# Row-tiled attention scores issued one batch pair ahead, with the odd units' softmax split over ScalarE and GpSimd

## The reference, cut to what matters

```python
x -> x + tanh(g_xattn[l]) * attention_l(layernorm(x), ctx)
x -> x + tanh(g_ffn[l])   * ffn_l(layernorm(x))          # layer 0: shared + top-1 of 8 experts; layer 1: two LoRA experts

scores = einsum('bhqd,bhkd->bhqk', Q, K) / sqrt(8)       # layer 1 adds a 64x64 bias and a key mask
attn = softmax(scores, -1)
out = einsum('bhqk,bhkd->bhqd', attn, V) @ Wo.T
```

## Time and profile before

| | us |
|---|---|
| median of 3 runs (lowest, highest) | 190.31 (189.04, 190.61) |
| the profiled execution, its own time | 189.79 |
| its span, first to last instruction | 188.0 |
| attention of layer 0 on DVE, unit 0 to the last norm before the tail | 13.58 to 55.5 |
| expert stage and what lies around it | 55.5 to 121.95 |
| attention of layer 1 on DVE, the same | 121.95 to 158.0 |
| rest of layer 1 (up- and down-projection, output) | 158.0 to 188.0 |

### The profile page before, as it was taken

The page is one execution under the profiler, slowest core; times in us unless marked ns, Lnnn a source line. Parts: engine busy times, 40 slices in busy tenths (PEclk is TensorE's granted clock), DMA queues, the critical chain, the costliest instruction groups (busy, mean ns, idle before and its releaser), DMA issues.

```text
span 188.0 us, 4325 instructions
## 1 busy us (share of the span) xinstructions
PE 171.0 (91%) x1606; PEld 94.8 (50%) x1606; DVE 145.8 (78%) x364; ACT 79.9 (43%) x178; POOL 78.4 (42%) x88
## 2 busy tenths in 40 slices
PE   8768599999998979899998969989999998998994
PEld 2234236555576446366665923333555555643593
DVE  0599997889989799385666496799989996869942
ACT  3253284664473342255554002245544556255300
POOL 8729991004043864005666603255674454110000
PEclk9999969999999999999999997999999999999999
DMA  6999999940002010444421030000000000000012
GB/s 158 321 420 362 257 239 247 207 137 2 3 0 24 29 58 31 89 105 91 78 51 31 6 111 4 0 2 2 3 0 3 0 3 0 3 0 0 3 40 71
DMA packets 19558, 15.01 MB, mean 80 GB/s; under 512 B 3493, under 2 KB 18087, under 8 KB 19282
## 3 DMA queue, kind: packets, MB, share of 16 engines
q1 hardware_dynamic: 18370, 13.17, 27.9%
q0 software_dynamic: 736, 1.07, 1.8%
q10 hardware_dynamic: 432, 0.50, 1.1%
HBM read 7.82 MB, written 6.85 MB: 78 GB/s over the span
## 4 chain that ended last, share of the span: by engine, by line
PE 53%; DVE 26%; issue 7%; DMA 5%; POOL 5%; ACT 2%; SPq 0%; DVEq 0%; POOLq 0%
PE bank L877 44%; PE bank L954 6%; DMA xr<-x_in 3%; POOL rstd L311 3%; DVE oT L640 2%; DVE Sa L633 2%; DVE xn L585 2%; POOL Sx L384 2%; DVE st L566 2%; PE bank L1193 2%; DVE Vx L606 2%; DVE mx L635 2%; DMA sorted_rows<-Pe,slot 1%; DVE QT L614 1%; DMA big<-sorted_rows 1%
## 5 line engine op out<-in xcount | busy, mean ns | idle before, releaser
L877 PE MATMUL bank<-Kx,QT 128*64 128x512 f32 x128 | 34.9, 629 | 2.6 <-DVE Sx L626 2.0
L311 POOL TENSOR_TENSOR rstd<-ve,nhalf 128x2 f32<-128x2 f32 x16 | 11.7, 728 | 54.1 <-DVE ve L572 54.0
L461 ACT ACTIVATE Pe<-Sx 128x512 f32<-128x512 f32 x32 | 20.2, 630 | 27.3 <-POOL Sx L384 15.1
L954 PEld LDWEIGHTS bank<-cst,Pe 128*128 128x128 f32 x128 | 13.8, 143 | 25.1 <-issue 14.6
L372 POOL DMA_INDIRECT routed_rows<-big x15 | 14.8, 984 | 19.3 <-DVE big L842 12.2
L465 ACT ACTIVATE big<-bank 128x512 f32<-128x512 f32 x32 | 18.8, 587 | 8.5 <-PE bank L954 8.2
L954 PE MATMUL bank<-cst,Pe 128*128 128x128 f32 x128 | 21.4, 291 | 0.7 <-ACT Pe L461 0.6
L384 POOL TENSOR_TENSOR Sx<-Sa,mx 128x512 f32<-128x512 f32 x16 | 16.8, 1049 | 11.3 <-DVE mx L635 11.3
L640 DVE RECIPROCAL oT<-bank 128x128 f32<-128x128 f32 x16 | 15.3, 953 | 3.7 <-PE bank L877 3.6
L877 PE MATMUL bank<-zb 128*32 128x512 bf16 x47 | 15.5, 473 | 2.5 <-DVE bo L597 1.4
L414 ACT ACTIVATE xn<-xr,nmr,rstd 128x128 f32<-128x128 f32 x20 | 9.1, 486 | 16.0 <-DVE nmr L578 16.0
(11 more groups left out here) (110 smaller groups left out, 302.9 us busy)
## 6 DMA issues: line engine op xcount, KB each, us to landing
sorted_rows<-empty SPq DMA_DIRECT2D x1, 4686.0 KB, 29.0
wgu<-rgu SPq DMA_DIRECT2D x1, 2048.0 KB, 10.6
wdn<-rdn SPq DMA_DIRECT2D x1, 1024.0 KB, 12.6
big<-sorted_rows SPq DMA_DIRECT2D x15, 66.0 KB, 1.9
ctxT<-ctx_in SPq DMA_DIRECT2D x2, 256.0 KB, 4.7
xr<-x_in SPq DMA_DIRECT2D x2, 256.0 KB, 5.3
wf<-ffn SPq DMA_DIRECT2D x1, 512.0 KB, 4.4
Kx<-KT SPq DMA_DIRECT2D x16, 32.0 KB
```

The costliest lines, as they stand in the source:

```text
L311: pool.tensor_tensor(rstd[:, w], ve[:, w], nhalf[:, w], ALU.pow).then_inc(s_pow, 1)
L461: act.activation(Pe[:, u % 3, :], Sx[:, u % 2, :], ACT.Exp).then_inc(s_exp, 1)
L877: return pe.matmul(o, l, r, start=first, stop=last, **k)
L954: ins = pe.transpose(bank[2 + u % 2][:, m * P:(m + 1) * P], Pe[:, u % 3, m * P:(m + 1) * P], ident)
```

## The change

**Scores.** K is now kept in four copies (`Kx` [P, 4, T]) and Q in one (`QT` [P, T]). The 16 heads are four groups of 32 features; a matmul contracts only one group's 32 rows with 256 streamed columns (4 heads). A unit is four such matmuls (two groups by two batches), which lie in different rows and columns of the array. The banks 0 to 3 become two double banks `pair0` and `pair1`; a unit's two groups end in two neighbouring banks, and `heads[i]` is the middle 512 columns.

**Order.** PE issues both units of pair n+1 ahead of the transposes of unit (n-1, odd) and (n, even), then the values of pair n-1 and out_proj of n-2. There is one bank for values, one for out_proj and one for each parity of transposes.

**Even units** are treated as before. **Odd units**: ACT copies the scores to `Sa` (`score_evac`); in layer 1 POOL adds bias and mask in place (`add_bias`); DVE takes the maximum in SBUF (`max_o`); POOL subtracts (`subtract`) in both layers. In layer 1 POOL subtracts for the even units too, as before.

**Other moves.** Both `v_proj` of layer 0 and `out_bias` stand ahead of the first scores. The transposes of xn pieces 2 and 3 and one `q_proj` of 512 columns for both come in iteration 2. The routed rows `xs` have a tile of their own. The last odd unit's transposes come behind `xn_transpose(q, 0)`. One `keep_warm` of two matmuls at the start of attention of layer 1 is gone.

```diff
@@ tensor
+            def scores(layer, n, hh):
+                if n >= 1:
+                    if hh == 1:
+                        pe.wait_ge(s_ev, PAIRS * layer + n)
+                    elif layer == 0:
+                        pe.wait_ge(s_sube, n)
+                    else:
+                        pe.wait_ge(s_adde, n)
+                for g in range(2):
+                    w = slice(32 * (2 * hh + g), 32 * (2 * hh + g + 1))
+                    for r in range(2):
+                        b = 2 * n + r
+                        o = pair[hh][S * r:S * r + S, 256 * (g + 1):256 * (g + 2)]
+                        ins = mm(o.rearrange("p (h k) -> p h k", h=HG), QT[w, b * S:(b + 1) * S],
+                                 Kx[w, :, b * S:(b + 1) * S])
+                ins.then_inc((s_Se, s_So)[hh], 1)
...
             def attention(layer, step):
+                for n in range(-1, PAIRS):
+                    if n < PAIRS - 1:
...
+                        scores(layer, n + 1, 0)
...
+                        scores(layer, n + 1, 1)
+                    if n == 2:
+                        xn_transpose(2 * layer, 2)
+                        xn_transpose(2 * layer, 3)
+                    if n >= 1:
+                        transposes(layer, n - 1, 1)
+                    if n >= 0:
+                        transposes(layer, n, 0)
+                    if n == 2:
+                        q_proj(layer, 2, 2)
+                    if n >= 1:
+                        values(layer, n - 1)
+                    if n == 3:
+                        out_proj(layer, 0)
+                    if n >= 3:
+                        out_proj(layer, n - 2)
+                xn_transpose(q, 0)
...
+                    pe.wait_ge(s_xnT, PIECES * q + 1)
+                    keep_warm(XT_BANK[q][0], 3)
+                    transposes(1, 7, 1)
+                    out_proj(1, 6)
+                    values(1, 7)
+                    xn_transpose(q, 1)
@@ vector
+                for n in range(PAIRS):
+                    unit_e(layer, n)
+                    if n in (4, 6):
+                        add_out(layer, n // 2 - 2)
...
+                    if n >= 2:
+                        norm(layer, n - 2)
+                    max_o(layer, n)
+                    if n == 0:
+                        q_evac(layer, 1)
+                        normalise(2 * layer, 2 + layer)
...
+                    if n == 2:
+                        q_evac(layer, 2, 2)
+                    if n in (4, 6):
+                        out_stats(layer, n // 2 - 2)
@@ gpsimd, layer 1
+            add_bias(0)
+            for n in range(PAIRS):
+                if n >= 1:
+                    subtract(1, n - 1, 1)
+                if n in (2, 3):
+                    residual_base(1, n - 2)
+                if n in (5, 7):
+                    rstd_of(3, (n - 5) // 2)
+                subtract(1, n, 0)
+                if n < PAIRS - 1:
+                    add_bias(n + 1)
+            subtract(1, PAIRS - 1, 1)
@@ scalar
+                for n in range(PAIRS):
+                    if n >= 1:
+                        exp(layer, n - 1, 1)
+                    if layer == 0:
+                        exp(0, n, 0)
+                    if n < PAIRS - 1:
+                        score_evac(layer, n + 1)
+                    if layer == 1:
+                        exp(1, n, 0)
...
+                    if n >= 1:
+                        pt_evac(layer, n - 1, 1)
...
+                    pt_evac(layer, n, 0)
...
+                    if n == 7:
+                        xnT_evac(q, 0)
...
+                            normalise(q, 1)
+                exp(layer, PAIRS - 1, 1)
+                pt_evac(layer, PAIRS - 1, 1)
```

More of the change, by code:

```diff
@@ L763, in attention @@
                 else:
-                    norm(1, 6)
-                    residual(1, 2)
                     norm(1, 7)
@@ L1078, in _ @@
             pe.wait_ge(d_cst, 32)
-            for a in (0, 1):
-                xn_transpose(0, a)
-                q_proj(0, a)
+            xn_transpose(0, 0)
+            q_proj(0, 0)
+            xn_transpose(0, 1)
+            v_proj(0, 0)
+            q_proj(0, 1)
+            v_proj(0, 1)
             def shared_up(n, halves=(0, 1)):
```

438 lines of the change are left out of this document (212 added, 226 removed).

## The result

| | median, us | lowest to highest | executions |
|---|---|---|---|
| before | 190.09 | 188.90 to 191.31 | 20 |
| changed | 191.80 | 190.41 to 193.94 | 20 |

The changed kernel takes 1.0077 times as long as before, 95% interval 1.0046 to 1.0108. Forecast were 186.3 us and a range of 182.0 to 191.3. The sign was wrong, and the time lies outside the range: it is 5.5 us above the forecast. The profiled execution took 192.07, with a span (first to last instruction) of 190.3 us.

What follows compares the result with a forecast made beforehand. PE (91% busy) bounded the kernel, DVE the first pairs of each layer. Span 188.0 - 5.6 + 0.1 + 0.4 + 1.0 = 183.9, plus 1.8 outside and 0.5 for the median: 186.2, said 186.3; range 182.0 to 191.3.

Steps and rivals of the forecast that it cites:

- The scores: PE in attention: a pair's scores take 0.75 us instead of 2.02, with bounds of 0.65 and 2.02.
- Rival B: Row groups do not run side by side, a pair's scores keep 2.02 us; 190.3 to 191.5 us; chance 0.13.
- DVE, ACT and POOL: Work per pair: DVE 3.15 us instead of 3.9, ACT about 2.6, POOL 3.3 in layer 1 with additions at 1.28.
- Rival D: PE remains the bound and the whole saving of 20 us arrives, 170 us; chance 0.02.
- Layer 0: Attention of layer 0: last maximum ends at 48.8 us, last residual at 56.5 instead of 62.1, a gain of 5.6.
- the walk: Step-by-step reckoning of both layers' attention, with pairs at 3.2 us in layer 0 and 3.4 in layer 1.
- the clock term: First pairs of both layers: light PE work brings 1.2 GHz; 1.0 us taken, +2.0 if counted in both layers.
- rival C: Clock stays low as PE waits for POOL or DVE; 3.4 us more per pair, two give 193.1; chance 0.12.
- Layer 1: Attention of layer 1: slow first three pairs, last norm at 154.8 instead of 158.0, tail gives it back; +0.1, addition +0.4.
- list of signs: What the profile after should show, among it layer 1's up-projections about 41 us behind its first unit.
- The Q copy and the tail: DVE gap of about 2 us ahead of the 512-column Q copy; last odd exponential on ACT behind xn's copy and layer norm.

Runs made afterwards that it cites:

- e11: e8 with every score matmul issued three times into the same place; 201.92 us, 1.0656 of the kernel before.
- e13: Changed kernel with idle matmuls on zeros in PE's waits of layer 0 alone (start and tail); 189.77 us, 1.0019 of the kernel before.
- e5: Changed kernel with idle matmuls on zeros in every place where PE waits, those of e1 and later pairs; 187.69 us, 0.9858 of before.
- e8: e7 with one layer norm tile in layer 1's first iteration moved from DVE to ACT; 184.41 us, 0.9692 of the kernel before.
- e1: Changed kernel with idle matmuls on zeros in the starts of both layers and the tail of layer 0; 190.31 us, 0.9977 of before.
- e2: Changed kernel with idle matmuls on zeros in layer 1's start only; 192.03 us, 1.0050 of the kernel before.
- e6: e5 with layer 1's last odd unit let ahead on ACT and PE, as in e4; 186.16 us, 0.9795 of the kernel before.
- e7: e6 with DVE's copy of 512 Q columns moved behind the even unit of pair 3; 184.99 us, 0.9722 of the kernel before.
- e4: Changed kernel with layer 1's last odd exponential and transposes let ahead, no idle matmuls added; 191.10 us, 1.0019 of the kernel before.
- e9: Changed kernel with only the later copy of 512 Q columns on DVE, no idle matmuls added; 190.61 us, 0.9982 of the kernel before.

## Why the prediction was wrong, point by point

**The scores, right.** 0.75 us per pair was taken; 0.61 at full clock. Rival B, no effect of the row tiling, is out by the timeline and by e11.

**DVE, ACT and POOL, right in their sizes.** The addition on POOL takes 1.27, taken at 1.28. In a pair without a residual, DVE's even unit comes 3.11 us after the one before (29.85 to 32.96), forecast 3.2 to 3.5. With a residual it is 5.3 to 6.0 (42.06 to 47.34 and 32.96 to 38.95), where 3.2 + 1.45 and small waits were counted. Rival D, PE stays the bound, is out: PE is busy 81% of the span.

**Layer 0, right except for the clock.** With the clock held the last residual starts at 56.49 (e13), 56.33 (e5) and 55.87 (e8); the walk said 56.5. In the changed kernel it starts at 60.68. Timeline of DVE in the changed kernel:

```profile
49.85 0.68 DVE L714 TENSOR_REDUCE mx<-Sa 128x8 f32<-128x512 f32 x1
...
60.68 0.48 DVE L728 SCALAR_TENSOR_TENSOR xr<-bank,tg,xb 128x256 f32<-128x256 f32 x1 [0.91 <-PE bank L956]
```

The last maximum ends at 50.53, 1.7 after the 48.8 of the walk; from there to the residual it takes 10.2 instead of 7.7. So 1.7 us were lost in the pairs and 2.5 in the tail, where the clock term had nothing. With the clock held both terms of the walk come out: in e5 the last maximum ends at 48.01 + 0.68 = 48.69, and the residual follows 7.6 us later.

**The clock, the step that failed.** It was put at +1.0, at most +2.0, for pair 0 of each layer, because PE's light work was looked for only where the walk showed long waits. Fillers bring back 4.1 us (e5): the term is that size. Three things were missed. The low clock also follows the tail of layer 0, where PE works in small pieces. It lasts longer than one stretch: against rival C stood that PE would be busy nearly all the time at half clock and so get the full clock back, but from 121.8 on in layer 1 PE was busy only 1.12 and 2.47 of 3.40 us at 1.2 GHz, waiting for DVE and POOL, and the low clock went on to 132.1. (the earlier trace rows do not show the clock behind their busy stretch either; the page's row of forty slices does.) And it isn't fixed in place: with PE idle 19% of the span, the low clock appears here or there (e1, e2, e13). Rival C named the right mechanism and gave it 0.12, with a price of 3.4 us for 6.8 us at 1.2 GHz, that is 0.5 us for each. In the later pairs the runs come near that: the 3.4 us stretch of e1 at 145.80 makes the step from unit_e(6) to unit_e(7) 152.82 - 145.44 = 7.4 us instead of 150.46 - 144.59 = 5.9 in e5, 0.4 us for each. In layer 1's start ten us at 1.2 GHz cost only 0.8, because others set the pace there. Over the whole kernel, 24 us cost about 4.1, a third of C's price.

**Layer 1, the second miss.** (unit_e(n) is the even unit of pair n on DVE.) The walk had unit_e(1), unit_e(2) and unit_e(3) 3.6, 6.2 and 13.5 us after the first unit. They came after 5.3, 7.9 and 16.3 (starts at 119.80, 125.06, 127.68, 136.07). From unit_e(3) to the up-projections, 28.3 + 0.4 = 28.7 was forecast, and it took 28.8. So the 2.8 us lie in the first three pairs, and 1.7 of them ahead of unit_e(1). There the clock has no part: in e6, at full clock, unit_e(1) also comes 121.48 - 116.21 = 5.3 us after the first unit. What was in no step of the walk is that POOL holds up two small DVE instructions, 1.05 and 0.80 us over their free durations. Taking one away brings unit_e(1) 1.06 us forward, of which 0.6 to 0.7 reach the end (e8); the other was not taken away in any run. The clock has 16.3 - 15.4 = 0.8: in e6 unit_e(3) comes at 131.64 - 116.21 = 15.4. The remaining 0.3 has no run of its own. The prediction's list of signs had about 41 us for this stage, its own walk 42.2; 45.03 was measured.

**The Q copy and the tail, right, and avoidable.** A gap of about 2 us ahead of the Q copy was forecast; 2.15 and 1.60 were seen, and the exponential behind the copy of xn's transposes too. Both were taken as given by the change. They are an order of instructions, and moving them gives 1.2 and 1.5 us with the clock held (e7, e6).

**The sum.** Of the 5.5 us between 186.3 and 191.8, the clock has about 3.1 (4.1 less the 1.0 that was counted), and the held DVE instructions up to 1.7. The rest, 0.7 or more, no run accounts for: of the one instruction that was moved only 0.6 of 1.06 us reached the time. The range failed for the same reason. Its upper end came from rival B, which does nothing to the clock, and C, which does, was left outside.

| version | us | ratio to before | last residual, layer 0 | first unit to up-projection, layer 1 |
|---|---|---|---|---|
| before | 190.09 | 1 | 62.12 | 40.71 |
| changed | 191.80 | 1.0077 | 60.68 | 45.03 |
| e5, clock held | 187.69 | 0.9858 | 56.33 | 44.83 |
| e6, and tail order | 186.16 | 0.9795 | 56.17 | 42.72 |
| e7, and later Q copy | 184.99 | 0.9722 | 55.96 | 41.93 |
| e8, and a norm tile on ACT | 184.41 | 0.9692 | 55.87 | 41.20 |

**What stays open.** The change as it was made loses 0.8%; with the clock held it gains 1.4%, and with three small moves more 3.1%. No run here tells why the stretch from 53.5 to 56.9, with PE busy in many small matmuls (2.49 of 3.40 us), was followed by 1.2 GHz, since the fillers of layer 0 were only tried together. Nor is it known which fillers of e5 are needed; those of one layer alone (e2, e13) and those of the starts and the tail (e1) bring back 2.0 us at most.

## What to carry to other kernels

When a change takes work from a PE that was nearly always busy (91% here), price the clock as its own term over the whole kernel, and not only at the longest wait: here light work in the two attention stages cost 4.1 us, more than the 2.4 us that the change gains with the clock held, and matmuls of zeros placed inside PE's existing waits brought it back. Then look at every in-order engine for an instruction that waits with ready work behind it, as the Q copy and the last exponential did; each was worth over 1 us with the clock held, for a few moved lines. Try such edits together with the held clock, since alone they stand in the spread that the clock makes (3.7 us in e4, 4.3 in e9, 0.5 in e7).
